# Attention over edges on one core: where the fade factors lie, and who makes two small results

## The chip, the cores and the metric

One core of a Trainium2 chip runs the whole program in one launch. The metric is the device time of one execution in microseconds. The kernel before was timed three times: 3548.37, 3549.31 and 3552.37 us, median 3549.31.

The engines are TensorE (PE; its weight loads are PEld), VectorE (DVE), ScalarE (ACT), GpSimd (POOL) and SyncE (SP). Each works through its own list of instructions in order and waits on semaphores for the others.

## The reference, cut to what matters

The program is four graph layers, each with a residual and a layer norm. The inputs are 50000 nodes of 128 features and 25000 edges sorted by destination. The third layer, a graph attention with 8 heads and a feed-forward part, is the one that the change touches:

```python
Q = (x @ Wq + bq).reshape(n, H, HD)
K = (x @ Wk + bk).reshape(n, H, HD)
V = (x @ Wv + bv).reshape(n, H, HD)
attn = jnp.sum(Q[dst] * K[src], axis=-1) * scale + edge_bias[edge_type]
mx = jax.ops.segment_max(attn, dst, num_segments=n)
ex = jnp.exp(attn - mx[dst])
sm = jax.ops.segment_sum(ex, dst, num_segments=n)
a = ex / (sm[dst] + 1e-16)
out = jax.ops.segment_sum(a[..., None] * V[src], dst, num_segments=n)
out = out.reshape(n, D) @ Wo + bo
x = _layernorm(x + out, g1, be1)
ffn = jax.nn.gelu(x @ W1 + b1, approximate=False) @ W2 + b2
return _layernorm(x + ffn, g2, be2)
...
x = _layernorm(x + _L2_gnn_ref(x, edge_index, edge_type_8, ...), axis=-1)
```

## The kernel before, in words

The stages run one after the other: a prelude, the node layer with the first edge layer, the PNA edges, the attention edges (`attention_edges`, from L2106) and the message edges. The attention stage starts near 2560 us of the profile and ends near 3240.

It takes the edges in 49 groups of 512, from the last group to the first. Since the edges are sorted by destination, the segment operations are scans along the 512 columns of a tile of 128 features by 512 edges. The softmax is kept running along the scan. PEAK (L2363) scans the running maximum, DIFFER (L2369) makes the gap between the running maximum of the neighbour and this edge's logit, and ACT splits the gap by sign. ABOVE (L2291) takes its positive part, BELOW (L2294) the negative part turned round. Both are put through exp(-x) by EXP_PROB (L2297) and EXP_FADE (L2300). The first gives the edge's weight, `prob`; the second gives the fade factor by which the sum so far is multiplied. SUM_PROB (L2379) and SUM_VALUES (L2385) then scan sum = fade * sum + new, once for the weights (`den`) and once for weights times values (`acc`).

In the kernel before, the logits lie in a PSUM bank named `bank_fade` (a_bfade in the profile). BELOW writes its result over them into the same bank, EXP_FADE works in place there, and both sums read the bank. So LOGITS on PE (L2234 to L2240) may write the next group's logits only when both sums of the group before are done, and waits for them.

Behind the sums come: the turn of `den` into rows (TURN_SUM), its reciprocal (INVERT, L2390 and L2393), WIDEN (L2304, ACT), DIVIDE (L2398), the product with Wo, RESIDUAL (L2402), a norm (SQUARE on ACT, SUM on DVE as an_var, ROOT on POOL as an_rstd, SCALE on ACT, L268), the feed-forward part with a norm of its own (FF_SUM as ai_var, FF_ROOT as ai_rstd on POOL, FF_SCALE on DVE, L2412), JOIN with the group's own rows (L2419), and the last norm. The last norm's MOMENTS on DVE are four bn_stats, four bn_aggr (al_mv) and one addition of eps (al_var, L252); LAST_ROOT on POOL raises al_var to the power -1/2 (al_rstd); SHIFT on DVE (al_shift, L297) and LAST on ACT (L305) use it. The own rows with a bias, `x2bT`, are made by BIAS_OWN on ACT (L2314) for OWN_ROWS on PE.

POOL also fetches the source rows: four indirect DMAs per group (FETCH0 to FETCH3, L1603), each of 128 rows, whose indices lie in SBUF. HOT (L2199) on POOL makes the one-hot rows of the edge types, and CARRY (L2203) copies one column.

The order of the work is written out by hand. Every step has a time in the list `AT`, PERIOD is 13.5, and each engine takes its steps in the order of their time modulo the period (`Flow`, `pipelined`). Tiles exist in two slots, and a step of a slot waits for what last used it. On POOL the order in a period is: BIAS_OWN's place (40.6 modulo 13.5 is 0.1), CARRY, FETCH0, HOT, LAST_ROOT, FETCH1, ROOT, FETCH2, FF_ROOT, FETCH3. On DVE: INVERT, JOIN, PEAK, DIVIDE, DIFFER, MOMENTS, RESIDUAL, SPREAD_OWN, SHIFT, WEIGH, SUM, SUM_PROB, FF_SUM, SUM_VALUES, MATCH, FF_SCALE.

Of the kernel before, what the change touches and what calls it, by code (L numbers as in the profile page):

```python
# [164 lines left out]
def backward(ap):  # L165

    return ap[:, ::-1]
# [34 lines left out]
class Norm:  # L202
# [40 lines left out]
    def moments(self, dve, i, s, y):  # L243

        for t in range(TPG):
            dve.bn_stats(self.st[s][:, t, :], y[:, t * P:(t + 1) * P]).then_inc(self.stats_made[s], 1)
        wait(dve, self.stats_made[s], i * 2 * TPG + TPG)
        self.mem.settle(dve)
        for t in range(TPG):
            dve.bn_aggr(self.mv[s][:, t, :], self.st[s][:, t, :]).then_inc(self.stats_made[s], 1)  # L250
        wait(dve, self.stats_made[s], i * 2 * TPG + 2 * TPG)
        dve.tensor_scalar(self.var[s][:], self.mv[s][:, :, 1], EPS, None, ALU.add).then_inc(self.summed[s], 1)  # L252

    def root(self, pool, i, s, j, minus_half):
        wait(pool, self.summed[s], self.nth(i, j))
# [1851 lines left out]
def attention_edges(nc, A, D, W, Ed, plan):  # L2107
# [6 lines left out]
    src, own, srcT, ownT, q, qk, gap, prob, pv, den, acc, o = (rows(n) for n in (  # L2114
        "src", "own", "srcT", "ownT", "q", "qk", "gap", "prob", "pv", "den", "acc", "o"))
    yT, n, nT, h, n2, x2bT, y3, x3, broad = (rows(name) for name in ("yT", "n", "nT", "h", "n2", "x2bT", "y3", "x3", "broad"))
    peak, inv = rows("peak", GROUP + 1), rows("inv", TPG * HEADS)
    low, keep = rows("low", GROUP, BF16), rows("keep", GROUP, BF16)
    typ = [mem.sb(f"a_typ{s}", [3 * TYPES, GROUP], I32) for s in range(S)]
    hot = [mem.sb(f"a_hot{s}", [3 * TYPES, GROUP], BF16) for s in range(S)]  # L2120

    bank_src, bank_own, bank_v, bank_fade, bank_y, bank_x = (mem.ps("a_b" + n) for n in ("src", "own", "v", "fade", "y", "x"))
    bank_ff = [mem.ps(f"a_bff{s}") for s in range(S)]
    outer, inner = Norm(mem, "an", S, 1), Norm(mem, "ai", S, 1)
    last = Norm(Mem(nc), "al", S, 1, squares=False, stats=True)
# [31 lines left out]
    with nc.Block() as block:  # L2157
# [29 lines left out]
        @block.gpsimd  # L2187
        def _(pool):
            pool.wait_ge(began, 2 * S + 4)

            def step(k, s, i):
                if k == FETCH0:
                    wait(pool, src_turned[s], i)
                if k in FETCH:
                    gsrc.tile(pool, s, FETCH.index(k), group(i, s))
                if k == HOT:
                    wait(pool, types_loaded[s], 16 * i + 16)
                    wait(pool, logits[s], i)
                    pool.tensor_scalar(hot[s][:], typ[s][:], W.split[:, 0:1], None, ALU.is_equal).then_inc(hot_made[s], 1)  # L2199
                if k == CARRY:  # L2200
                    wait(pool, peaked[s - 1], before(i, s))
                    wait(pool, differed[s], i)
                    pool.tensor_copy(peak[s][:, GROUP:], peak[s - 1][:, 0:1]).then_inc(carried[s], 1)  # L2203
                if k == ROOT:
                    outer.root(pool, i, s, 0, W.minus_half)
                if k == FF_ROOT:
                    inner.root(pool, i, s, 0, W.minus_half)
                if k == LAST_ROOT:
                    last.root(pool, i, s, 0, W.minus_half)

            pipelined(pool, plan.EG, S, PERIOD, AT, step, tail=rounds)

        @block.tensor
        def _(pe):
            def step(k, s, i):
# [18 lines left out]
                if k == LOGITS:  # L2234
                    wait(pe, hot_made[s], i + 1)
                    wait(pe, matched[s], i + 1)
                    wait(pe, prob_summed[s - 1], before(i, s))
                    wait(pe, values_summed[s - 1], before(i, s))
                    pe.matmul(bank_fade[:], W.head_bias[:], hot[s][:], start=True, stop=False)
                    pe.matmul(bank_fade[:], W.heads[:], qk[s][:], start=False, stop=True).then_inc(logits[s], 1)  # L2240
                if k == TURN_SUM:
                    wait(pe, prob_summed[s], i + 1)
                    wait(pe, outer.normed[s - 1], before(i, s))
# [32 lines left out]
        def _(act):  # L2276
            def step(k, s, i):
                if k == COPY_SRC:
                    wait(act, src_turned[s], i + 1)
                    wait(act, k_made[s], i)  # L2280
                    wait(act, v_made[s], i)
                    act.copy(srcT[s][:], bank_src[:]).then_inc(src_copied[s], 1)
                if k == MOVE_Q:
                    wait(act, q_made[s], i + 1)
                    wait(act, matched[s], i)
                    act.activation(q[s][:], bank_own[:], ACT.Identity, bias=BQc).then_inc(q_moved[s], 1)
                if k == ABOVE:
                    wait(act, differed[s], i + 1)
                    wait(act, prob_summed[s], i)
                    wait(act, weighed[s], i)  # L2290
                    act.activation(prob[s][:], gap[s][:], ACT.Relu).then_inc(split[s], 1)  # L2291
                if k == BELOW:
                    wait(act, differed[s], i + 1)
                    act.activation(bank_fade[:], gap[s][:], ACT.Relu, scale=-1.0).then_inc(split[s], 1)  # L2294
                if k == EXP_PROB:
                    wait(act, split[s], 2 * i + 2)
                    act.activation(prob[s][:], prob[s][:], ACT.Exp, scale=-1.0).then_inc(exped[s], 1)  # L2297
                if k == EXP_FADE:
                    wait(act, split[s], 2 * i + 2)
                    act.activation(bank_fade[:], bank_fade[:], ACT.Exp, scale=-1.0).then_inc(exped[s], 1)  # L2300
                if k == WIDEN:
                    wait(act, inverted[s], 2 * i + 2)
                    wait(act, spread[s], i)
                    act.copy(broad[s][:].rearrange("p (h d) -> p h d", d=P // HEADS), over(inv[s][:], P // HEADS)).then_inc(widened[s], 1)  # L2304
                if k == SQUARE:
                    wait(act, y_made[s], i + 1)
                    outer.square(act, i, s, 0, tiles(bank_y[:]))
                if k == SCALE:
                    wait(act, n_turned[s], i)
                    outer.scale_by_scalar(act, i, s, 0, n[s], bank_y)  # L2310
                if k == BIAS_OWN:
                    wait(act, own_spread[s], i + 1)
                    wait(act, x_turned[s], i)
                    act.activation(x2bT[s][:], ownT[s][:], ACT.Identity, bias=W.c_be2[:, 0:1]).then_inc(biased[s], 1)  # L2314
                if k == N_COPY:
                    wait(act, n_turned[s], i + 1)
                    act.copy(nT[s][:], bank_ff[s][:]).then_inc(n_copied[s], 1)
                if k == GELU:
                    wait(act, hidden[s], i + 1)
                    act.activation(h[s][:], bank_ff[s][:], ACT.Gelu, bias=W.b1_ffn[:, 0:1]).then_inc(gelued[s], 1)  # L2320
                if k == EVICT:
                    wait(act, ff_made[s], i + 1)
                    act.activation(nT[s][:], bank_ff[s][:], ACT.Identity, bias=W.c_ffn[:, 0:1]).then_inc(evicted[s], 1)
                if k == FF_SQUARE:
                    wait(act, ff_turned[s], i + 1)
                    inner.square(act, i, s, 0, tiles(bank_ff[s][:]))
                if k == LAST:
                    wait(act, stored[s], 16 * i)
                    last.scale_moments_by_scalar(act, i, s, 0, x3[s], y3[s])
# [4 lines left out]
        def _(dve):  # L2334
# [7 lines left out]
            def step(k, s, i):  # L2342
# [14 lines left out]
                if k == PEAK:  # L2357
# [2 lines left out]
                    wait(dve, peaked[s - 1], before(i, s))  # L2360
                    wait(dve, carried[s - 1], before(i, s))
                    wait(dve, differed[s], i)
                    dve.tensor_tensor_scan(backward(peak[s][:, 0:GROUP]), backward(bank_fade), backward(low[s]), peak[s - 1][:, 0:1],  # L2363
                                           ALU.max, ALU.add).then_inc(peaked[s], 1)
                if k == DIFFER:
                    wait(dve, peaked[s], i + 1)
                    wait(dve, carried[s], i + 1)
                    wait(dve, split[s], 2 * i)
                    dve.tensor_tensor(gap[s][:], peak[s][:, 1:], bank_fade[:], ALU.subtract).then_inc(differed[s], 1)  # L2369
                if k == WEIGH:  # L2370
                    wait(dve, v_made[s], i + 1)
                    wait(dve, exped[s], 2 * i + 1)
# [2 lines left out]
                if k == SUM_PROB:  # L2375
                    wait(dve, exped[s], 2 * i + 2)
                    wait(dve, prob_summed[s - 1], before(i, s))
                    wait(dve, sum_turned[s], i)
                    dve.tensor_tensor_scan(backward(den[s]), backward(bank_fade), backward(prob[s]), den[s - 1][:, 0:1],  # L2379
                                           ALU.mult, ALU.add).then_inc(prob_summed[s], 1)  # L2380
                if k == SUM_VALUES:
                    wait(dve, exped[s], 2 * i + 2)
                    wait(dve, weighed[s], i + 1)
                    wait(dve, values_summed[s - 1], before(i, s))
                    dve.tensor_tensor_scan(backward(acc[s]), backward(bank_fade), backward(pv[s]), acc[s - 1][:, 0:1],  # L2385
                                           ALU.mult, ALU.add).then_inc(values_summed[s], 1)
                if k == INVERT:
                    wait(dve, sum_turned[s], i + 1)
# [30 lines left out]
                    dve.tensor_tensor(y3[s][:], n2[s][:], bank_x[:], ALU.add).then_inc(joined[s], 1)  # L2419
                if k == MOMENTS:  # L2420
                    wait(dve, joined[s], i + 1)
                    last.moments(dve, i, s, y3[s])
                if k == SHIFT:
                    last.shift_moments(dve, i, s, 0)

# [253 lines left out]
```

## Time and profile before

| | |
|---|---|
| runs, median | 3549.31 us (3548.37 to 3552.37) |
| profiled execution, span from first to last instruction | 3856.9 us |
| mean granted TensorE clock over the span | 0.885 |
| busy over the span | PE 79%, DVE 71%, ACT 60%, POOL 65% |
| busy from 2800 to 2900 us (100 us of the attention stage) | PE 92.01, PEld 50.62, DVE 96.96, ACT 95.59, POOL 68.82 us |
| granted clock from 2800 to 2900 us | 1.00 |

The profiled execution is one execution, recorded with its instructions; only its span is known, not what lies around it. It is 307.6 us longer than the median of the runs shown. Times of rows are therefore those of this execution.

### The profile page before, as it was taken

What the parts mean: (1) busy time and instruction counts of PE and PEld (TensorE: products, weight loads), DVE (VectorE), ACT (ScalarE), POOL (GpSimd) and SP (SyncE); (2) the same over time, 40 slices, a digit from 0 to 9 for tenths busy, and PEclk for the clock granted to TensorE, in tenths of its full rate; (3) what the DMA queues carried; (4) which work ended last, traced back from release to release, by engine and by line L of the source; (5) the groups of instructions that cost most, each with busy time, mean ns of one, the idle gap of its engine ahead of it and who ended that gap; (6) DMA issues with size and microseconds to landing.
All of it is one profiled execution on the core that took longest, in us unless ns stands there. A gap on an engine that the chain in (4) does not pass through costs nothing. (4 is left out here: it accounts for less than half of the span.)

```text
span 3856.9 us, 54369 instructions
## 1 busy us (share of the span) xinstructions
PE 3033.4 (79%) x11490; PEld 2023.8 (52%) x11490; DVE 2725.5 (71%) x6900; ACT 2299.0 (60%) x5259; POOL 2523.9 (65%) x2721
## 2 busy tenths in 40 slices
PE   3124149999999998899979999979999996777676
PEld 2012035555555555777759999955555553343333
DVE  3005749999999998777769989969999994222222
ACT  2003039999999999777623333439999994232332
POOL 5750069999999998777534444436666763666665
PEclk7557569999999999899989999989999997777777
DMA  5012025555555554444323343322322321222221
GB/s 190 1 36 90 1 76 171 171 168 169 171 164 175 164 176 141 113 123 119 109 86 112 114 112 110 109 81 72 88 83 84 86 82 44 72 73 72 72 68 46
DMA packets 262118, 404.65 MB, mean 105 GB/s; under 512 B 61938, under 2 KB 104135, under 8 KB 262033
## 3 DMA queue, kind: packets, MB, share of 16 engines
q1 hardware_dynamic: 204920, 304.18, 24.6%
q0 software_dynamic: 44032, 73.90, 8.4%
q10 hardware_dynamic: 13081, 25.69, 2.0%
q14 instruction: 62, 0.51, 0.0%
q8 instruction: 23, 0.38, 0.0%
HBM read 213.15 MB, written 194.37 MB: 106 GB/s over the span
## 5 line engine op out<-in xcount | busy, mean ns | idle before, releaser
L256 POOL TENSOR_TENSOR dn_rstd<-dn_var,w_minus_half 128x4 f32<-128x4 f32 x294 | 292.6, 1002 | 16.7 <-DVE dn_var L241 16.5
L1603 POOL DMA_INDIRECT m_src<-table_x,e_src_first x196 | 191.1, 975 | 127.5 <-issue 52.1
L1603 POOL DMA_INDIRECT p_src<-table_x,e_src x196 | 213.1, 1087 | 93.0 <-issue 53.6
L2491 POOL DMA_INDIRECT out_rows<-m_x,e_out_first x196 | 197.6, 1008 | 94.0 <-issue 65.8
L648 POOL DMA_INDIRECT scratch_node_row<-o_own,e_out x196 | 192.0, 979 | 90.7 <-issue 62.4
L1643 POOL DMA_INDIRECT g_own<-in_x,e_dst x196 | 223.9, 1142 | 36.9 <-issue 36.9
L2576 DVE TENSOR_TENSOR m_y<-m_bout,m_own 128x512 f32<-128x512 f32 x49 | 33.9, 692 | 294.3 <-DMA a_typ<-in_type_row 166.3
L1603 POOL DMA_INDIRECT a_src<-table_x,e_src x196 | 200.9, 1025 | 47.6 <-issue 37.5
L1634 POOL DMA_INDIRECT g_src<-scratch_wide,e_src x196 | 192.0, 980 | 58.8 <-issue 46.0
L1409 PE MATMUL n_banks<-w_gru_both,d_xT 128*128 128x256 f32 x784 | 223.6, 430 | 8.6 <-ACT d_xT L1446 8.6
L1409 PEld LDWEIGHTS n_banks<-w_gru_both,d_xT 128*128 128x128 f32 x784 | 192.9, 327 | 71.3 <-ACT d_xT L1446 68.6
L1970 POOL TENSOR_TENSOR pn_rstd<-pn_var,w_minus_half 128x4 f32<-128x4 f32 x49 | 51.1, 1043 | 256.9 <-DVE pn_var L241 256.9
L237 ACT ACTIVATE dn_sq<-n_banks 128x512 f32<-128x512 f32 x294 | 180.2, 614 | 62.2 <-DVE n_banks L1550 46.6
L925 ACT COPY s_xT<-s_bturn 128x512 f32<-128x512 f32 x98 | 52.3, 592 | 269.1 <-remote 222.0
L241 DVE TENSOR_REDUCE dn_var<-dn_sq 128x4 f32<-128x516 f32 x294 | 199.6, 680 | 17.6 <-issue 10.3
L2524 PE MATMUL m_bhid<-m_mx,w_w1b 128*128 128x512 f32 x98 | 80.8, 919 | 116.5 <-DVE m_mx L2570 65.2
L1824 PE MATMUL n_banks<-w_own,d_n 128*128 128x384 f32 x392 | 165.6, 572 | 0.0
L2000 PE MATMUL p_bout<-w_post,p_mx 128*128 128x384 f32 x392 | 165.0, 503 | 0.0
L305 ACT ACTIVATE d_x<-d_y,dl_shift,dl_rstd 128x128 f32<-128x128 f32 x392 | 161.7, 486 | 0.0
L2000 PE MATMUL p_bout<-w_post,p_mn 128*128 128x384 f32 x392 | 158.8, 487 | 0.0
L2000 PE MATMUL p_bout<-w_post,p_mean 128*128 128x384 f32 x392 | 158.5, 486 | 0.0
L2000 PE MATMUL p_bout<-w_post,p_var 128*128 128x384 f32 x392 | 158.5, 486 | 0.0
(486 smaller groups left out, 9952.8 us busy)
## 6 DMA issues: line engine op xcount, KB each, us to landing
table_x<-d_x SPq DMA_DIRECT2D x294, 256.0 KB, 2.0
g_src<-in_x_wide SPq DMA_DIRECT2D x97, 262.0 KB
scratch_wide<-g_src SPq DMA_DIRECT2D x97, 262.0 KB
out_rows<-d_x SPq DMA_DIRECT2D x97, 256.0 KB
s_x<-in_x ACTq DMA_DIRECT2D x31, 768.0 KB
table_x<-d_xT SPq DMA_DIRECT2D x49, 256.0 KB
scratch_post<-d_x SPq DMA_DIRECT2D x49, 256.0 KB, 2.0
p_rc<-scratch_rcount SPq DMA_DIRECT2D x49, 256.0 KB
```

What stands on the lines that cost most here:

```text
L237: act.activation(self.sq[s][:, :, 0:P], y, ACT.Square, scale=ROOT).then_inc(self.squared[s], 1)
L241: dve.tensor_reduce(self.var[s][:], self.sq[s][:], AX, ALU.add).then_inc(self.summed[s], 1)
L256: pool.tensor_tensor(self.rstd[s][:], self.var[s][:], minus_half[:], ALU.pow).then_inc(self.rooted[s], 1)
L305: ins = act.activation(out[:, c], y[:, c], ACT.Identity, bias=self.shift[s][:, t:t + 1], scale=self.rstd[s][:, t:t + 1])
L648: pool.indirect_dma_start(out=D["node_row"], out_offset=bass.IndirectOffsetOnAxis(ap=Ed.out[:, t:t + 1], axis=0), in_=self.own[:, t, :], i ...
L1409: mm = pe.matmul(pair[s][:, 2 * t * P:2 * (t + 1) * P], xT[s][:, t:GROUP:TPG], W.gru_both[:], start=True, stop=True, skip_group_check=True)
L1603: pool.indirect_dma_start(out=self.rows[s][:, t * P:(t + 1) * P], out_offset=None, in_=self.table, in_offset=bass.IndirectOffsetOnAxis(ap= ...
L1634: pool.indirect_dma_start(out=self.src[s][:, t, :], out_offset=None, in_=self.D["wide"], in_offset=bass.IndirectOffsetOnAxis(ap=self.Ed.sr ...
L1643: pool.indirect_dma_start(out=self.own[:, at * P:(at + 1) * P], out_offset=None, in_=self.A["x"], in_offset=bass.IndirectOffsetOnAxis(ap=s ...
L1824: mm = pe.matmul(wide(t), x1T[s][:, t:GROUP:TPG], W.own[:], start=False, stop=True, skip_group_check=True)
L2000: mm = pe.matmul(bank_out[:, t * GROUP:t * GROUP + SCALERS * P], cols[s][:, t:GROUP:TPG], W.post[:, stat_block(n, 0):stat_block(n, SCALERS ...
L2491: pool.indirect_dma_start(out=D["out"], out_offset=bass.IndirectOffsetOnAxis(ap=Ed.out_first[:, at:at + 1], axis=0), in_=x4[s][:, t * P:(t ...
```

## The change: what it does

- The logits keep a bank of their own, now named `bank_fit`. BELOW writes into a new SBUF tile, `fade`, one per slot, EXP_FADE works in place there, and SUM_PROB and SUM_VALUES read it there. BELOW gets a wait for the sums of two groups before; LOGITS waits for the gap of the group before instead of its two sums.
- BIAS_OWN is taken from ACT and given to POOL, with the same waits.
- The addition of eps for the last norm (al_var) is taken from DVE and given to POOL, ahead of the power in LAST_ROOT.
- `AT`, PERIOD and all else stay as they are.

```diff
         dve.tensor_scalar(self.var[s][:], self.mv[s][:, :, 1], EPS, None, ALU.add).then_inc(self.summed[s], 1)
+
+    def begin_moments(self, dve, i, s, y):
+
+        for t in range(TPG):
+            dve.bn_stats(self.st[s][:, t, :], y[:, t * P:(t + 1) * P]).then_inc(self.stats_made[s], 1)
+        wait(dve, self.stats_made[s], i * 2 * TPG + TPG)
+        self.mem.settle(dve)
+        for t in range(TPG):
+            dve.bn_aggr(self.mv[s][:, t, :], self.st[s][:, t, :]).then_inc(self.stats_made[s], 1)
+
+    def root_of_moments(self, pool, i, s, minus_half):
+
+        wait(pool, self.stats_made[s], i * 2 * TPG + 2 * TPG)
+        pool.tensor_scalar(self.var[s][:], self.mv[s][:, :, 1], EPS, None, ALU.add).then_inc(self.summed[s], 1)
+        self.root(pool, i, s, 0, minus_half)
...
     yT, n, nT, h, n2, x2bT, y3, x3, broad = (rows(name) for name in ("yT", "n", "nT", "h", "n2", "x2bT", "y3", "x3", "broad"))
+    fade = rows("fade")
     peak, inv = rows("peak", GROUP + 1), rows("inv", TPG * HEADS)
...
-    bank_src, bank_own, bank_v, bank_fade, bank_y, bank_x = (mem.ps("a_b" + n) for n in ("src", "own", "v", "fade", "y", "x"))
+    bank_src, bank_own, bank_v, bank_fit, bank_y, bank_x = (mem.ps("a_b" + n) for n in ("src", "own", "v", "fit", "y", "x"))
     bank_ff = [mem.ps(f"a_bff{s}") for s in range(S)]
...
                 if k == LAST_ROOT:
-                    last.root(pool, i, s, 0, W.minus_half)
+                    last.root_of_moments(pool, i, s, W.minus_half)
+                if k == BIAS_OWN:
+                    wait(pool, own_spread[s], i + 1)
+                    wait(pool, x_turned[s], i)
+                    pool.tensor_scalar(x2bT[s][:], ownT[s][:], W.c_be2[:, 0:1], None, ALU.add).then_inc(biased[s], 1)
...
                     wait(pe, matched[s], i + 1)
-                    wait(pe, prob_summed[s - 1], before(i, s))
-                    wait(pe, values_summed[s - 1], before(i, s))
-                    pe.matmul(bank_fade[:], W.head_bias[:], hot[s][:], start=True, stop=False)
-                    pe.matmul(bank_fade[:], W.heads[:], qk[s][:], start=False, stop=True).then_inc(logits[s], 1)
+                    wait(pe, differed[s - 1], before(i, s))
+                    pe.matmul(bank_fit[:], W.head_bias[:], hot[s][:], start=True, stop=False)
+                    pe.matmul(bank_fit[:], W.heads[:], qk[s][:], start=False, stop=True).then_inc(logits[s], 1)
                 if k == TURN_SUM:
...
                     wait(act, differed[s], i + 1)
-                    act.activation(bank_fade[:], gap[s][:], ACT.Relu, scale=-1.0).then_inc(split[s], 1)
+                    wait(act, values_summed[s], i)
+                    act.activation(fade[s][:], gap[s][:], ACT.Relu, scale=-1.0).then_inc(split[s], 1)
                 if k == EXP_PROB:
...
                     wait(act, split[s], 2 * i + 2)
-                    act.activation(bank_fade[:], bank_fade[:], ACT.Exp, scale=-1.0).then_inc(exped[s], 1)
+                    act.activation(fade[s][:], fade[s][:], ACT.Exp, scale=-1.0).then_inc(exped[s], 1)
                 if k == WIDEN:
...
                     outer.scale_by_scalar(act, i, s, 0, n[s], bank_y)
-                if k == BIAS_OWN:
-                    wait(act, own_spread[s], i + 1)
-                    wait(act, x_turned[s], i)
-                    act.activation(x2bT[s][:], ownT[s][:], ACT.Identity, bias=W.c_be2[:, 0:1]).then_inc(biased[s], 1)
                 if k == N_COPY:
...
                     wait(dve, differed[s], i)
-                    dve.tensor_tensor_scan(backward(peak[s][:, 0:GROUP]), backward(bank_fade), backward(low[s]), peak[s - 1][:, 0:1],
+                    dve.tensor_tensor_scan(backward(peak[s][:, 0:GROUP]), backward(bank_fit), backward(low[s]), peak[s - 1][:, 0:1],
                                            ALU.max, ALU.add).then_inc(peaked[s], 1)
...
                     wait(dve, split[s], 2 * i)
-                    dve.tensor_tensor(gap[s][:], peak[s][:, 1:], bank_fade[:], ALU.subtract).then_inc(differed[s], 1)
+                    dve.tensor_tensor(gap[s][:], peak[s][:, 1:], bank_fit[:], ALU.subtract).then_inc(differed[s], 1)
                 if k == WEIGH:
...
                     wait(dve, sum_turned[s], i)
-                    dve.tensor_tensor_scan(backward(den[s]), backward(bank_fade), backward(prob[s]), den[s - 1][:, 0:1],
+                    dve.tensor_tensor_scan(backward(den[s]), backward(fade[s]), backward(prob[s]), den[s - 1][:, 0:1],
                                            ALU.mult, ALU.add).then_inc(prob_summed[s], 1)
...
                     wait(dve, values_summed[s - 1], before(i, s))
-                    dve.tensor_tensor_scan(backward(acc[s]), backward(bank_fade), backward(pv[s]), acc[s - 1][:, 0:1],
+                    dve.tensor_tensor_scan(backward(acc[s]), backward(fade[s]), backward(pv[s]), acc[s - 1][:, 0:1],
                                            ALU.mult, ALU.add).then_inc(values_summed[s], 1)
...
                     wait(dve, joined[s], i + 1)
-                    last.moments(dve, i, s, y3[s])
+                    last.begin_moments(dve, i, s, y3[s])
                 if k == SHIFT:
```

## Rows read from the trace of the kernel before

**Rows 1.** Tile view of a_gap: count, ns min/median/max, first and last start.
```profile
L2369 DVE TENSOR_TENSOR a_gap<-a_peak,a_bfade x49: 679/681/689, 2574.8 to 3197.2; 128x512 f32<-128x512 f32 x49
```

**Rows 2.** Timeline of DVE, one period: start us, us, engine, line, operation.
```profile
2900.36 0.38 DVE L250 BATCH_NORM_AGGREGATE al_mv<-al_st 128x2 f32<-128x6 f32 x4 [0.15 <-DVE al_st L246]
2900.77 0.52 DVE L252 TENSOR_SCALAR al_var<-al_mv 128x4 f32<-128x4 f32 x1
2900.85 0.75 DVE L2402 SCALAR_TENSOR_TENSOR a_yT<-a_by,w_c_bo,a_ownT 128x512 f32<-128x512 f32 x1
...
2902.93 0.14 DVE L297 SCALAR_TENSOR_TENSOR al_shift<-al_mv,al_rstd 128x4 f32<-128x4 f32 x1
...
2903.65 0.68 DVE L241 TENSOR_REDUCE an_var<-an_sq 128x4 f32<-128x516 f32 x1
2904.24 1.27 DVE L2379 TENSOR_TENSOR_SCAN a_den<-a_bfade,a_den,a_prob 128x512 f32<-128x512 f32 x1
...
2906.01 1.27 DVE L2385 TENSOR_TENSOR_SCAN a_acc<-a_bfade,a_acc,a_pv 128x512 f32<-128x512 f32 x1
...
2907.85 1.12 DVE L2412 SCALAR_TENSOR_TENSOR a_n<-a_bff,ai_rstd,w_g 128x128 f32<-128x128 f32 x4
```

**Rows 3.** Timeline of ACT, the same period (in brackets: idle before it, releaser).
```profile
2899.45 0.63 ACT L2291 ACTIVATE a_prob<-a_gap 128x512 f32<-128x512 f32 x1 [0.29 <-DVE a_gap L2369]
2899.99 0.58 ACT L2294 ACTIVATE a_bfade<-a_gap 128x512 f32<-128x512 f32 x1
...
2902.99 0.59 ACT L237 ACTIVATE an_sq<-a_by 128x512 f32<-128x512 f32 x1
2903.47 0.60 ACT L2300 ACTIVATE a_bfade<-a_bfade 128x512 f32<-128x512 f32 x1
...
2905.55 1.14 ACT L268 ACTIVATE a_n<-a_by,an_rstd 128x128 f32<-128x128 f32 x4
...
2908.57 0.74 ACT L2314 ACTIVATE a_x2bT<-a_ownT,w_c_be 128x512 f32<-128x512 f32 x1
2909.48 0.62 ACT L2304 COPY a_broad<-a_inv 128x512 f32<-128x512 f32 x1 [0.18 <-DVE a_inv L2393]
```

**Rows 4.** Timeline of POOL, the same period.
```profile
2899.68 1.59 POOL L2199 TENSOR_SCALAR a_hot<-a_typ,w_split 24x512 bf16<-24x512 int32 x1
2901.37 1.05 POOL L256 TENSOR_TENSOR al_rstd<-al_var,w_minus_half 128x4 f32<-128x4 f32 x1
...
2904.41 1.04 POOL L256 TENSOR_TENSOR an_rstd<-an_var,w_minus_half 128x4 f32<-128x4 f32 x1 [0.69 <-DVE an_var L241]
2905.65 1.02 POOL L1603 DMA_INDIRECT a_src<-table_x,e_src  x1 [0.20 <-issue]
2906.70 1.05 POOL L256 TENSOR_TENSOR ai_rstd<-ai_var,w_minus_half 128x4 f32<-128x4 f32 x1
...
2911.25 0.18 POOL L2203 COPY a_peak<-a_peak 128x1 f32<-128x1 f32 x1 [2.29 <-DVE a_peak L2363]
```

**Rows 5.** Groups by line of POOL: count, busy us, mean ns, idle before.
```profile
L1519 POOL TENSOR_TENSOR d_x2b<-d_x,w_be 128x512 f32<-128x512 f32 x98 | 126.5, 1291 | 3.5 <-DVE d_y L1572 0.9
```

**Rows 6.** Timeline of DVE and POOL in the node stage, around 567 us.
```profile
566.98 0.70 DVE L1555 TENSOR_TENSOR n_banks<-d_x,w_bo 128x512 f32<-128x512 f32 x1 [0.78 <-ACT d_x L1458]
567.09 1.50 POOL L256 TENSOR_TENSOR dl_rstd<-dl_var,w_minus_half 128x4 f32<-128x4 f32 x1
```

**Rows 7.** Timeline of DVE and POOL in the PNA stage, around 2210 us.
```profile
2209.80 1.26 DVE L2068 TENSOR_TENSOR_SCAN p_s<-p_keep,p_s,p_sqr 128x512 f32<-128x512 bf16 x1
...
2209.12 0.95 POOL L1603 DMA_INDIRECT p_src<-table_x,e_src  x1 [0.30 <-issue]
2210.38 1.44 POOL L1603 DMA_INDIRECT p_src<-table_x,e_src  x1 [0.30 <-issue]
```

**Rows 8.** Timeline of DVE and POOL in the node stage, around 806 us.
```profile
806.30 0.17 DVE L252 TENSOR_SCALAR dl_var<-dl_mv 128x4 f32<-128x4 f32 x1
...
806.13 1.00 POOL L256 TENSOR_TENSOR do_rstd<-do_var,w_minus_half 128x4 f32<-128x4 f32 x1
```

## What the change will do to the time

> **What bounds the kernel now.** The change touches one stage only, the attention over 49 groups of 512 edges, so I read that stage and not the page's totals. The chain of waits covers under a fifth of the span and names none of its lines, so it decides nothing here. I went first to the gap's instruction over the whole stage: 49 of them, the first at 2574.8 us and the last at 3197.2 [rows 1]. That is 622.4 us for 48 steps, 12.97 us per group. Then I read one steady period engine by engine, in order of time.
>
> VectorE (DVE) [rows 2]: nearly every instruction starts before the one ahead of it has ended. a_den starts at 2904.24 while an_var runs to 2904.33. So DVE has next to nothing to give. ScalarE (ACT) [rows 3]: it stands still twice, and both times for DVE, 0.29 us before ABOVE (waits for a_gap) and 0.18 us before WIDEN (waits for a_inv). GpSimd (POOL) [rows 4]: it has holes, 0.69 us before ROOT and 2.29 us before CARRY, but two of its results arrive just in time. ai_rstd ends at 2907.75 and FF_SCALE, its reader on DVE, starts at 2907.85. an_rstd ends at 2905.45 and SCALE on ACT starts at 2905.55.
>
> One more edge is tight. SQUARE on ACT ends at 2903.58 and an_var on DVE starts 0.07 us later [rows 2, 3]. So two loops have the same length: all of DVE's list, and a_gap, ABOVE, BELOW, table load, EXP_PROB, EVICT, SQUARE, back to an_var. A third hangs on the first: an_var, then on POOL ROOT, one fetch (FETCH2) and FF_ROOT, then FF_SCALE.
>
> **The change part by part.**
>
> *al_var from DVE to POOL.* It starts at 2900.77 and the next instruction 0.08 us later, but it also waits for the last of four al_mv aggregations, which begin at 2900.36 and end at 2900.74 [rows 2]. Without it RESIDUAL could start behind the fourth one's begin, near 2900.66, not at 2900.85: DVE gains 0.19 us. On POOL it stands between HOT and LAST_ROOT. Its cost there lies between 0.18 us (the copy for CARRY) and 1.05 us (the power on 128x4) [rows 4]. I take 0.2, since it is an addition as cheap as the copy, and 0.1 for the wait between the two. al_rstd then ends near 2902.72, still ahead of SHIFT at 2902.93 (2902.74 if DVE is 0.19 earlier); FETCH1 moves 0.3 us later, into the 0.69 us hole before ROOT. At 1.05 us SHIFT would wait some 0.7 us, 0.7 x 48 = 34 us.
>
> *BIAS_OWN from ACT to POOL.* ACT loses 0.74 us, but just behind it ACT waits for DVE's a_inv anyway [rows 3], so nothing comes of it directly. On POOL it falls into the 2.29 us hole before CARRY. Its price is bounded by the two nearest streams over 512 columns, 1.29 us for a two-input addition [rows 5] and 1.59 for HOT [rows 4]; either fits, and its reader OWN_ROWS is a period and more behind. No wait follows: cost 0.
>
> *The fade factors in SBUF, ACT's side.* BELOW reads the same gap as ABOVE and writes PSUM, 0.58 us against 0.63 for ABOVE's write into SBUF [rows 3]. It will cost 0.05 more, on the loop through SQUARE. So the 0.19 us saved on DVE doesn't shorten the period, because that loop is as long, and the 0.05 lengthens it: +0.05 us. EXP_FADE gets some 0.03 longer and ends near 2904.15, still ahead of a_den.
>
> *LOGITS' waits.* In place of the two sums of the group before it waits for that group's gap, done earlier. It sits behind MATCH, whose DVE instruction follows a_acc, so the old wait ended nothing: 0.
>
> *The fade factors in SBUF, DVE's side.* This is the part that decides. Today a_den and a_acc read one operand from PSUM (a_bfade) and one from SBUF. Afterwards both come from SBUF. What POOL does beside such an instruction the trace shows in other stages. dl_rstd, the same power on 128x4, began 0.11 us into L1555, whose inputs d_x and w_bo are both in SBUF. It took 1.50 us in place of the 1.05 of [rows 4] and ended 0.91 us behind L1555's end [rows 6]. A fetch that began in the scan of p_sqr and p_keep, both in SBUF, with 0.68 us of it to go, took 1.44 us; the one before it, which began under the scan that reads a bank, took 0.95 [rows 7]. So POOL waited for the end of the DVE instruction in both, by about 0.45 and 0.49. Today ROOT begins 0.17 us into a_den and FF_ROOT 0.69 us into a_acc, at 1.04 and 1.05 us each [rows 2, 4]: a scan with one bank operand holds nothing up.
>
> Step by step for the period shown, in the changed kernel:
> 1. a_den 2904.24 to 2905.51, both operands in SBUF. ROOT is released by an_var at 2904.41, so always inside the scan. It ends 0.91 behind the scan: 2906.42, not 2905.45 (+0.97).
> 2. FETCH2 begins 0.20 later, 2906.62. a_acc runs 2906.01 to 2907.28, so 0.66 us is to go: 1.02 + 0.49 = 1.51 us, end 2908.13, not 2906.67.
> 3. FF_ROOT 2908.17 to 2909.22.
> 4. FF_SCALE on DVE at 2909.32, not 2907.85: +1.47 us.
> ACT's SCALE starts 0.97 later, but with BIAS_OWN gone and WIDEN itself 1.47 later it catches up. PE's TURN_SUM stands behind N_TURN, which waits for SCALE, and is needed at INVERT, which is 1.47 later too. The relief on ACT is worth something here: it keeps this shift from spreading.
>
> Sum per period: 1.47 + 0.05 = +1.52 us. Fetches run for all but the last groups, which gives about 45 periods with ROOT, FETCH2 and FF_ROOT in a row; in three more, with no fetch between, FF_ROOT waits about 0.4. 45 x 1.52 + 3 x 0.4 = 70 us on the profiled execution, whose span is 3856.9 us. The runs' median is 3549.3, 0.92 of it, and nothing in the page tells where the rest lies; scaled by it 70 becomes 64. Forecast 3549.3 + 64 = 3614 us, unscaled 3619.
>
> A page goes further than these rows. The Trainium skill, "SBUF — State Buffer", section "Who interferes with whom", says that a VectorE instruction with two SBUF inputs contends with a GpSimd instruction that reads SBUF, and that whoever is first has the shared ports for its whole length. The first half is what [rows 6, 7] show. The second half is only half seen: al_var, begun under HOT, ended at 2901.29 with HOT (2901.27), 0.52 us long [rows 2, 4]; but dl_var, begun 0.17 us into a power, took 0.17 [rows 8]. I go by the rows: a power reads its few elements early and holds nobody afterwards.
>
> **The rivals.**
> - *POOL holds DVE too.* If ROOT holds the read path to its end at 2906.42, a_acc starts then and ends at 2907.69; FETCH2 ends at 2908.54, FF_ROOT at 2909.63, FF_SCALE at 2909.73: +1.88. (1.88 + 0.05) x 45 + 1 = 88, scaled 81: 3630 us. Against it: [rows 8].
> - *Only ROOT is held*, the fetch gets its addresses before a_acc matters: +0.97, (0.97 + 0.05) x 45 + 1 = 47, scaled 43: 3592 us. Against it: [rows 7].
> - *BIAS_OWN holds DVE.* As HOT held al_var, it could hold a_inv's reciprocal (SBUF to SBUF), which lands on it, by up to 1.2 us more: (1.52 + 1.2) x 46 = 125, scaled 115: 3665 us. No row shows a reciprocal held.
> - *Nothing is held.* If EXP_FADE ends after 2904.34, ROOT reads first; or a scan doesn't hold a power. Then BELOW's 0.05 x 48 = 2.4 is left: 3551.5 us. Against it: EXP_FADE ended at 2904.07 [rows 3], and with 0.08 more it stays ahead of that point.
> - *Faster.* DVE's list alone sets the period (the 0.07 us behind SQUARE being chance), and the reads don't collide. The point from which it decides is SQUARE's end: were it 0.19 us earlier relative to DVE, which the missing BIAS_OWN would have to bring about, DVE's gain would count: 0.19 x 48 = 9.1, scaled 8.4: 3541 us. Against it: [rows 6] and ACT's wait for a_gap.
>
> **How the numbers follow.** Forecast 0.58, POOL holds DVE 0.10, only ROOT 0.12, BIAS_OWN 0.06, nothing held 0.08, faster 0.06. 0.2% of this time is 7 us, about what a measurement can tell from none. Slower 0.58 + 0.10 + 0.12 + 0.06 = 0.86, same 0.08, faster 0.06. The forecast's own range is 3595 to 3630. The range for 8 in 10 leaves out the last two and BIAS_OWN's case: 3560 to 3645; its lower part is for a POOL chain with more room in the timed runs than in the profile, its upper part for al_var at 1.05 us on POOL.
>
> **What would show it.** an_rstd near 2.0 us long in place of 1.04, and the fetch behind it near 1.5, with the other three fetches unchanged; a new wait of DVE at L2412 for ai_rstd, over 1 us in most periods; the gap's instructions some 14.4 us apart; al_rstd still 1.05. al_var at POOL over 0.5 us, or a reciprocal over 0.4, would show the other prices. an_rstd at 1.04 us would make the prediction wrong at its root.

## The result, and the profile after

The changed kernel takes 3618.21 us (median of 4 runs, 3616.15 to 3625.55) against 3550.26 (4 runs, 3548.37 to 3552.37): ratio 1.0195, 95% interval 1.018 to 1.0209, 68 us slower. Its profiled execution has a span of 3617.4 us.

Tile view of a_gap of the kernel after; it answers to [rows 1]. 48 steps now take 687.0 us, 14.31 each in place of 12.97: 64.6 of the 68 us lie here. TensorE's granted clock is no rival: its mean over the stage is 1.00 of full speed before (2575 to 3197 us) and 0.99 after (2361 to 3047).
```profile
L2385 DVE TENSOR_TENSOR a_gap<-a_peak,a_bfit x49: 678/681/687, 2360.6 to 3047.6; 128x512 f32<-128x512 f32 x49
```

Timeline of DVE, one period, to be laid beside [rows 2] (start us, us, engine, line, operation; in brackets the idle time before it and who ended it): a_den and a_acc now read a_fade, and a_n (FF_SCALE) waits 1.30 us for POOL.
```profile
2705.39 0.38 DVE L261 BATCH_NORM_AGGREGATE al_mv<-al_st 128x2 f32<-128x6 f32 x4 [0.15 <-DVE al_st L257]
2705.69 0.72 DVE L2418 SCALAR_TENSOR_TENSOR a_yT<-a_by,w_c_bo,a_ownT 128x512 f32<-128x512 f32 x1
...
2708.69 0.69 DVE L241 TENSOR_REDUCE an_var<-an_sq 128x4 f32<-128x516 f32 x1
2709.29 1.27 DVE L2395 TENSOR_TENSOR_SCAN a_den<-a_fade,a_den,a_prob 128x512 f32<-128x512 f32 x1
...
2711.07 1.27 DVE L2401 TENSOR_TENSOR_SCAN a_acc<-a_fade,a_acc,a_pv 128x512 f32<-128x512 f32 x1
2712.26 0.73 DVE L2372 SCALAR_TENSOR_TENSOR a_qk<-a_bsrc,w_cols,a_q 128x512 f32<-128x512 f32 x1
2714.28 1.13 DVE L2428 SCALAR_TENSOR_TENSOR a_n<-a_bff,ai_rstd,w_g 128x128 f32<-128x128 f32 x4 [1.30 <-POOL ai_rstd L271]
```

Timeline of ACT, the same period [rows 3]: the standstill before WIDEN (a_broad) has grown from 0.18 to 1.29 us, and SCALE (a_n) waits 0.78 for an_rstd.
```profile
2701.59 0.62 ACT L2324 COPY a_broad<-a_inv 128x512 f32<-128x512 f32 x1 [1.29 <-DVE a_inv L2409]
...
2705.03 0.61 ACT L2314 ACTIVATE a_fade<-a_gap 128x512 f32<-128x512 f32 x1
...
2708.07 0.59 ACT L237 ACTIVATE an_sq<-a_by 128x512 f32<-128x512 f32 x1
...
2711.50 1.14 ACT L283 ACTIVATE a_n<-a_by,an_rstd 128x128 f32<-128x128 f32 x4 [0.78 <-POOL an_rstd L271]
```

Timeline of POOL, the same period [rows 4]: ROOT is released at 2709.46, 0.17 us into a_den, and takes 1.95 us. FETCH2 behind it begins under a_acc and takes 1.56. FF_ROOT is as long as before but ends late. From here on I call an instruction of POOL held when it takes longer because a scan of DVE beside it has not ended. In the whole stage 48 of the 49 ROOTs are held.
```profile
2701.16 1.59 POOL L2229 TENSOR_SCALAR a_x2bT<-a_ownT,w_c_be 128x512 f32<-128x512 f32 x1
...
2706.34 0.24 POOL L266 TENSOR_SCALAR al_var<-al_mv 128x4 f32<-128x4 f32 x1
...
2709.46 1.95 POOL L271 TENSOR_TENSOR an_rstd<-an_var,w_minus_half 128x4 f32<-128x4 f32 x1 [0.47 <-DVE an_var L241]
2711.61 1.56 POOL L1618 DMA_INDIRECT a_src<-table_x,e_src  x1 [0.20 <-issue]
2713.20 1.05 POOL L271 TENSOR_TENSOR ai_rstd<-ai_var,w_minus_half 128x4 f32<-128x4 f32 x1
```

Waits of DVE from 2450 to 2950 us (us in total, times, longest). The row is the loss: 1.30 us in each period. In the kernel before no such row existed.
```profile
DVE a_n L2428 <- POOL ai_rstd L271: 45.4, 35, 1.3
```

### The profile page after: what moved, and what is told of

Its sections match the earlier page's. It is cut to its first block and busy times, and to the rows that moved or that the text cites. A ratio compares the mean times of both kernels' runs of the same rounds, so it can differ in the third digit from the quotient of the medians.

```text
span 3617.4 us, 54328 instructions
## 1 busy us (share of the span) xinstructions
PE 2983.9 (82%) x11490; PEld 2013.1 (56%) x11490; DVE 2728.8 (75%) x6851; ACT 2274.1 (63%) x5210; POOL 2683.0 (74%) x2819
## 5 line engine op out<-in xcount | busy, mean ns | idle before, releaser
L1618 POOL DMA_INDIRECT a_src<-table_x,e_src x196 | 227.6, 1161 | 47.9 <-issue 37.8
L1419 PE MATMUL n_banks<-w_ident,g_src 128*128 128x128 f32 x392 | 64.2, 287 | 102.3 <-DVE d_n L307 80.3
L1419 PEld LDWEIGHTS n_banks<-w_ident,g_src 128*128 128x128 f32 x392 | 42.0, 143 | 180.7 <-DVE d_n L307 79.9
```

The source lines that it names most:

```text
L1618: pool.indirect_dma_start(out=self.rows[s][:, t * P:(t + 1) * P], out_offset=None, in_=self.table, in_offset=bass.IndirectOffsetOnAxis(ap= ...
```

## The experiments

Each was timed beside the kernel before on one chip; ratios are to that. There the kernel before took 3555 to 3556.5 us and not 3550, so where an expectation names a time, what counts is its distance from the kernel before.

**One operand of one scan (the kernel before).**
```diff
-dve.tensor_tensor_scan(backward(den[s]), backward(bank_fade), backward(prob[s]), ...
+dve.tensor_tensor_scan(backward(den[s]), backward(prob[s]), backward(prob[s]), ...
```


> The kernel before with one operand changed: the a_den scan reads prob twice (both operands in SBUF) in place of the fade factors in the bank and prob. So the weights are summed with a wrong factor; ACT's writes, the a_acc scan and all waits stay as before. My theory, that the place of the scan's operands is what holds POOL: an_rstd 1.94 us long, the fetch behind it 1.02 (a_acc holds nobody), FF_SCALE 0.97 us later, less what ACT and the loads add: 46 x 0.97 = 45, 3600 us. Rival, that it is ACT's writes into SBUF or the new tile: an_rstd 1.04 us, 3555 us.

Measured 3600.96 us, ratio 1.0131 (1.0114 to 1.0148): 46 us more, where 45 had been expected. Here are its powers and fetches (ns min/median/max):
```profile
L256 POOL TENSOR_TENSOR an_rstd<-an_var,w_minus_half x49: 1007/1944/1947, 2379.0 to 3049.9; 128x4 f32<-128x4 f32 x49
```
```profile
L1603 POOL DMA_INDIRECT a_src<-table_x,e_src x196: 940/1017/1097, 2345.0 to 3014.1; - x196
```
Only that operand differs (it is the tile `prob` a second time, so the sums are wrong and the run serves for its times alone). an_rstd goes from 1.04 to 1.94 us in 48 of 49 groups, while ai_rstd stays at 1.05 us and the fetches, 46 of which begin under a_acc, at 1.02. ACT still writes into the bank, so its writes and the new tile are out as causes: it is where the scan's operands lie. The run also splits the loss: ROOT's hold alone is worth 46 us of the 68.

**The two halves of the change.** Moves only: BIAS_OWN and al_var on POOL, `bank_fade` as before. Fade only: the rest of the diff.

> The two moves alone (BIAS_OWN and al_var to GpSimd), the fade factors left in the bank. My theory: the two scans hold nobody, an_rstd takes 1.04 us, the fetch behind it 1.02, and the loop through SQUARE keeps the period at 12.97 us: 3550 us, at best 3541 if DVE's 0.19 us count. Rival, a busier GpSimd (1.59 + 0.24 us more per group) is what slowed the changed kernel: about 3618 us.

> The fade factors in SBUF alone, BIAS_OWN on ACT and al_var on DVE as before. My theory now: an_rstd 1.95 us, the fetch 1.56 us, FF_SCALE waits some 1.3 us; ACT stood still 1.29 us before WIDEN in the changed kernel, so BIAS_OWN's 0.56 us fits in: 3618 us, within 7. The rival is what I wrote in the prediction, that ACT's relief keeps the shift from spreading: up to 0.56 x 46 = 26 us more, 3644 us. The busier-GpSimd rival: about 3550.

Moves only: 3556.57 us, ratio 1.0002 (0.9991 to 1.0012). Fade only: 3619.59, ratio 1.018 (1.0158 to 1.0203). an_rstd is 1.04 us long in the first and 1.94 in the second, whose 48 steps take 688.1 us (687.0 in the changed kernel). So the loss is the fade tile's, and in this order of POOL's list the busier POOL costs nothing. The second run also fells a claim of the prediction: with BIAS_OWN back on ACT the time is the same. ACT still waits for a_inv there, some 0.7 us per period in place of 1.3; it had more room than the relief gave. Waits of ACT in the fade-only kernel (in these rows: us in total, times, longest):
```profile
ACT a_broad L2320 <- DVE a_inv L2409: 22.8, 34, 0.7
```

**The delay made by a semaphore (the kernel before).**
```diff
 if k == ROOT:
+    wait(pool, prob_summed[s - 1], min(i + 1 + s, in_slot(plan.EG, S, (s - 1) % S)))
     outer.root(pool, i, s, 0, W.minus_half)
```


> The kernel before, fade factors in the bank, but ROOT on GpSimd waits for the end of the a_den scan beside it. It makes by a semaphore the delay that I ascribe to the read path. My theory: ROOT starts 1.17 us later, an_rstd 1.04 us long, the fetch 1.02 us (not held), FF_SCALE 1.18 us later: 46 x 1.18 = 54, 3604 us. Rival, that delay on this chain is absorbed and the loss comes from elsewhere (the writes into SBUF, the longer powers' effect on DVE): under 3570 us.

3626.0 us, ratio 1.0202 (1.0179 to 1.0224), an_rstd 1.04 us long. A late ROOT is enough for a loss of this size, with the fade factors in the bank. I had it 16 us too low, 54 us where 70 were measured. Besides a_n DVE waits for PE, whose list stands behind SCALE on ACT, and SCALE waits for an_rstd (40.7 us in 35 periods, 27.3 in the changed kernel). That this makes the 16 us wasn't tried. Waits of DVE:
```profile
DVE a_n L2413 <- POOL ai_rstd L256: 36.6, 35, 1.1
DVE a_o L2399 <- PE a_by L321: 6.8, 8, 1.2
...
DVE a_ownT L2351 <- DMA a_keep<-scratch_keep: 4.6, 14, 0.9
```

**FETCH2 behind FF_ROOT (the changed kernel).**
```diff
-AT = (0, 13.4, 13.6, 13.7, 3, 6.4, 10.2, 12.5, ...
+AT = (0, 13.4, 13.6, 13.7, 3, 6.4, 11.6, 12.5, ...
```


> The changed kernel with FETCH2 put behind FF_ROOT on GpSimd. My theory: ROOT still ends 0.85 behind a_den, FF_ROOT then begins inside a_acc, is held to its end and ends 0.85 behind it, at 2713.19 in the times of the changed kernel's period shown, not at 2714.25: 0.99 us less per group, 3618 - 46 = 3572 us; ai_rstd 1.7 to 1.8 us long. Rival, a hold only of a power that is released during a_den: ai_rstd 1.05 us, DVE doesn't wait for it, 3550 us or a little above.

3599.67 us, ratio 1.0123 (1.0095 to 1.015): 43 us above the kernel before, where 22 had been expected. On POOL it went as written, two powers held one behind the other:
```profile
2704.28 1.94 POOL L271 TENSOR_TENSOR an_rstd<-an_var,w_minus_half 128x4 f32<-128x4 f32 x1 [0.54 <-DVE an_var L241]
2706.22 1.74 POOL L271 TENSOR_TENSOR ai_rstd<-ai_var,w_minus_half 128x4 f32<-128x4 f32 x1
```
But nearly half of what FF_SCALE gave back turned up at another place: 17.7 us for a_keep, where a_n's wait fell from 45.4 to 6.9. Waits of DVE from 2450 to 2950 us:
```profile
DVE a_ownT L2366 <- DMA a_keep<-scratch_keep: 17.7, 28, 1.5
DVE a_n L2428 <- POOL ai_rstd L271: 6.9, 36, 0.2
```
SyncE's issues show why. The load of a_keep is the third load behind a store (table_x) that waits for LAST on ACT in each period (36 waits), and LAST stands behind SCALE, which waits 1.16 us for an_rstd in the period shown:
```profile
2709.39 0.37 SPq L2197 DMA_DIRECT2D table_x<-a_x  x1
2710.10 0.33 SPq L2181 DMA_DIRECT2D a_own<-table_x  x1
2710.68 0.33 SPq L2189 DMA_DIRECT2D a_low<-scratch_low  x1
2711.41 0.33 SPq L2193 DMA_DIRECT2D a_keep<-scratch_keep  x1
```

**The same, with STORE behind the loads** (`80.9` to `81.5` at the end of `AT`).

> The kernel with FETCH2 behind FF_ROOT, and STORE put behind the loads on SyncE. There DVE waited 17.7 us in 36 periods for a_keep, whose load stands behind a store that waits for ACT's LAST, which ROOT's hold made late. If that is the whole of its miss (3600 measured, 3572 expected): the waits for a_keep go and 3600 - 17.7 x 46/36 = 3577 us is left. Rival, the load is late by itself or the miss has another cause: 3595 to 3600 us.

3591.1 us, ratio 1.0105 (1.0087 to 1.0122). The two intervals overlap, but the 48 steps of the traces take 656.5 us against 663.9: some 7 us less, not 22. The waits for a_keep are gone, and SHIFT waits instead. In this order POOL has no idle time before CARRY any more, so CARRY, FETCH0, HOT, al_var and LAST_ROOT come late behind FETCH3 and BIAS_OWN; here the work moved to POOL does stand on a path that DVE waits for:
```profile
DVE al_shift L312 <- POOL al_rstd L271: 9.7, 35, 0.3
DVE a_n L2428 <- POOL ai_rstd L271: 7.1, 37, 0.2
```

**WEIGH between SUM and SUM_PROB (the changed kernel),** so that ROOT begins under an instruction with one SBUF operand: in `AT` WEIGH 34.5 to 35.5, SQUARE 48.1 to 47.4.

> The changed kernel with WEIGH between SUM and SUM_PROB on DVE, and SQUARE ahead of EVICT on ACT so that SUM can come that early. ROOT then begins under WEIGH, which reads a bank and one SBUF tile. My theory, that a power is held only if it begins inside a scan of two SBUF operands: an_rstd 1.04 us, the fetch behind it 1.02, but FF_ROOT begins some 0.2 us inside a_acc and is held, 1.7 to 1.9 us long; period 13.46 us, 0.5 above the kernel before: 3550 + 23 = 3573 us. Rival, POOL is held in whatever part of its instruction the scan meets: an_rstd stays near 1.9, 3600 us or more.

3576.22 us, ratio 1.0058 (1.0041 to 1.0076): 21 us above the kernel before, expected 23. In its trace 47 of 49 ROOTs begin 0.34 to 0.49 us ahead of a_den, and though the scan then begins under them they take 1.01 to 1.06 us. So what decides is whether the scan is already under way when the power begins. **And MATCH between FF_SUM and SUM_VALUES** (25.5 to 24.2), for FF_ROOT:

> As the one with WEIGH between, and MATCH put between FF_SUM and SUM_VALUES, so that FF_ROOT too begins under an instruction with one SBUF operand. My theory: all three powers 1.05 us with the fade factors still in SBUF, period 13.08 us (DVE waits 0.3 us for SQUARE), 3555 us. Rivals: SBUF operands slow the scans or ACT's writes as such, then 3580 us or more is left; the hold meets the powers anyway, 3600.

3560.88 us, ratio 1.0014 (1.0003 to 1.0024): 5.5 us, expected 5. The powers of the first, then of the second:
```profile
L271 POOL TENSOR_TENSOR an_rstd<-an_var,w_minus_half x49: 1011/1059/1922, 2383.3 to 3026.6; 128x4 f32<-128x4 f32 x49
L271 POOL TENSOR_TENSOR ai_rstd<-ai_var,w_minus_half x49: 1007/1756/1913, 2398.2 to 3040.4; 128x4 f32<-128x4 f32 x49
```
```profile
L271 POOL TENSOR_TENSOR an_rstd<-an_var,w_minus_half x49: 1008/1057/1922, 2379.2 to 3011.4; 128x4 f32<-128x4 f32 x49
L271 POOL TENSOR_TENSOR ai_rstd<-ai_var,w_minus_half x49: 1006/1049/1912, 2393.7 to 3025.2; 128x4 f32<-128x4 f32 x49
```
The operands are still in SBUF in both. By order alone the ratio falls from 1.0195 to 1.0014. What is left isn't the powers: one ROOT of 49 began inside a_den after all (the maximum of 1922 ns), and two FF_ROOTs inside a_acc. Three things grew. DVE waits 9.5 us for a_keep (4.3 in the kernel before) and 3.6 for SQUARE in 38 periods, and the fetches that begin under a_den or a_acc, 91 of the 196, take some 1.2 us in place of 1.02. Which of them makes the 0.14% wasn't separated.

**In search of the gain of the moves.** The moves save DVE 0.19 us per group and yet bring nothing. Four runs look for what swallows it: moves only, with SQUARE ahead of EVICT; the store order (STORE behind the loads) alone in the kernel before; the moves with both; and the kernel with both between with that store order.

> The two moves without the fade part, and SQUARE ahead of EVICT on ACT. If the loop through SQUARE is what swallowed DVE's 0.19 us per group, it is now 0.5 us shorter and DVE's list alone decides: 12.97 - 0.19 = 12.78 us per group, 48 x 0.19 = 9 us under the kernel before, ratio 0.9975. Rival, the gain of the moves is lost elsewhere (SHIFT waiting for al_rstd, loads): ratio 1.000.

> The kernel before with STORE put behind the loads on SyncE, nothing else. DVE waited 4.3 us for a_keep in 38 periods; if those waits go, 4.3 x 48/38 = 5 us: ratio 0.9985. Rival: the loop through SQUARE gives none of it back, ratio 1.000.

> The two moves, SQUARE ahead of EVICT, fade factors in the bank, and STORE behind the loads on SyncE. Without the last of these DVE waited 13.5 us for a_keep in 38 periods, three times as long as in the kernel before, and the gain was nil. If that wait is where the gain of the moves went: 13.5 x 46/38 = 16 us less, ratio 0.9955. Rival: SHIFT's wait for al_rstd takes its place (that chain had 0.0 to 0.1 us to spare), ratio 0.999 or more.

> The changed kernel (fade factors in SBUF, the moves) with WEIGH and MATCH between, SQUARE ahead of EVICT, and STORE behind the loads. DVE waited 9.5 us for a_keep in 38 periods without the last of these: 9.5 x 46/38 = 11.5 us less, ratio 0.998. Rival: ROOT, late in some periods behind FETCH1, is held more often, ratio 1.001 or more.

Ratios: 1.0005 (0.9996 to 1.0014) with SQUARE first; 0.9987 (0.9978 to 0.9996) for the store order alone; 0.9983 (0.9974 to 0.9992) for the moves, SQUARE and store order together, 3549.44 us; 1.0017 (1.0008 to 1.0026) with both between and the store order. Waits of DVE with SQUARE first, and in the one with both between and the store order:
```profile
DVE a_ownT L2365 <- DMA a_keep<-scratch_keep: 13.5, 29, 1.5
```
```profile
DVE an_var L241 <- ACT an_sq L237: 7.8, 38, 0.2
```
In the first, the wait for a_keep is 13.5 us in 38 periods where the kernel before has 4.3, and these 9 us are more than the 7 that 0.19 us per group come to. With STORE last that wait goes, yet only half of the 16 us is gained: 12.85 us per group by the gap's view ((2981.1 - 2364.4) / 48), where the store order alone has 12.91. Here is a period of that kernel:
```profile
2700.80 1.05 POOL L271 TENSOR_TENSOR al_rstd<-al_var,w_minus_half 128x4 f32<-128x4 f32 x1
2701.88 0.16 DVE L312 SCALAR_TENSOR_TENSOR al_shift<-al_mv,al_rstd 128x4 f32<-128x4 f32 x1
2702.05 0.75 DVE L2389 SCALAR_TENSOR_TENSOR a_pv<-a_bv,w_cols,a_prob 128x512 f32<-128x512 f32 x1
```
SHIFT begins 0.03 us behind al_rstd's end, which had 0.51 us to spare with the store order alone. WEIGH (a_pv) then begins 0.17 us behind SHIFT's start; in the kernel before it came 0.05 behind it, at 2902.98 against 2902.93 [rows 2]. Over 37 periods that is 0.09 us per group on average, about half of the 0.19. Another 0.04 stands ahead of PEAK. That these delays come from al_rstd was not tested. In the last one the waits for a_keep were exchanged for waits for SQUARE, and nothing came of it. The store order alone does nearly as much as all together (the intervals overlap), so no gain of the moves is shown. The fastest kernel lies 0.17% below the kernel before, and with 0.9983 against 1.0195 some 2.1% below the changed one.

## Why the prediction was right

*The term that decides.* Steps 1 to 4 came as drawn. an_rstd ends 0.85 us behind a_den (I took 0.91), FETCH2 takes 1.56 us (1.51), FF_ROOT 1.05. From an_var's start to FF_SCALE's it was 4.20 us and is 5.59: +1.39 where I had 1.47. The one-operand run shows the cause, the two orders with an instruction between show that it takes a power that begins inside the scan, and the semaphore run shows that the delay is enough.

*BELOW in SBUF.* It takes 0.61 us, not 0.58: 0.03 more, I had 0.05. But the term didn't belong in the sum. From a_gap's start to an_var's it is 4.91 us in both periods shown: the 0.07 us that an_var stood behind SQUARE's end [rows 2, 3] took it up (0.03 now).

*The sum.* 1.52 x 45 + 1 = 70 us was within 2 of the measured 68, but partly by luck. The 48 steps grew by 64.6 us, 1.34 each, so the sum was 5 us too high where it counts. Of this 0.08 per period is the chain (1.39, not 1.47) and 0.05 is BELOW. I also left out that DVE's waits for a_keep (4.3 us in 38 periods of the kernel before) vanish when the period grows. The 3 us between 64.6 and 68 lie outside the steps; the fade-only kernel, whose steps are as long, was 63 us above the kernel before in its own comparison.

*The factor 0.92 was wrong.* It made 64 of the 70, and only by luck comes near the 64.6 of the steps. The 307.6 us by which the profiled execution exceeded the runs lie outside this stage. The first gap came at 2574.8 us [rows 1] against 2360.6 in the kernel after, 214 us later; from the last gap to the end it was 659.7 against 569.8 us, 90 more. The moves-only kernel's 48 steps take 622.3 us in a span of 3554.2, and [rows 1] gives 622.4 in one of 3856.9. The unscaled 3619 is 1 us off, the forecast 3614 is 4 off.

*al_var and BIAS_OWN.* 0.24 us on POOL (I took 0.2), and 1.59 us, the upper of my bounds, in the hole. No DVE instruction was held by it: the reciprocal is 0.35 us as before. As forecast the moves bring nothing. I gave the loop through SQUARE as the reason; the run with SQUARE first shows that it isn't the only one, since the loads' wait stands behind it.

*ACT's relief* was said to keep the shift from spreading. It doesn't; ACT has the room without it, as the fade-only run shows.

*The rivals.* POOL does not hold DVE for a power's whole length: a_acc starts at 2711.07 while the power runs to 2711.41, and takes 1.27 us. "Only ROOT is held" was priced at 47 us before the factor, and the one-operand run, where only ROOT is held, measured 46; by FETCH2's 1.56 us it isn't what the change does.

## What to carry to other kernels

Before an operand of a VectorE instruction goes from a bank into SBUF, look whether its other operand lies there too, and which GpSimd instruction is released while it runs. If that one's result is awaited just in time, its delay is the price. Putting an instruction with one SBUF operand between the two avoids it without a bank: here that brought 1.95% down to 0.14%. A gain on a full engine counts only when each chain that ends just in time (here SQUARE, a_keep's load and perhaps al_rstd) is as far ahead as the gain; check SyncE's list too, where a store that waits holds up the loads behind it.

## What the runs showed of the hardware

A power on 128x4 takes 1.04 us by itself and 1.94 to 1.95 when it begins 0.16 to 0.17 us into a scan of 1.27 us with two SBUF operands; it ends 0.83 to 0.85 us behind the scan (medians). FF_ROOT waits likewise where it begins inside a_acc: 1.74 us in the kernel with FETCH2 behind it. A power that began 0.34 us or more ahead of the scan isn't held: 1.06 us in the kernel with WEIGH between. An indirect fetch that begins under such a scan takes 1.56 us in place of 1.02. A scan itself is no slower with both operands in SBUF (1.27 us in both kernels), nor when a power is under way.

That a VectorE instruction with two SBUF inputs contends with GpSimd's reads is the rule of the Trainium skill ("SBUF — State Buffer", "Who interferes with whom"), and the one-operand run is a clean case of it. Its further words, that the first one has the ports for its whole instruction, fit what the scan did to the power, and not the power: a scan that began under a power took 1.27 us all the same.
